# Two GNN layers on one core: rows from one scratch, and the adjacency over three DMA queues

## What is computed

```python
h = relu(layernorm(x))
mask = (adj > 0); deg = sum(mask, axis=1)
agg = mask @ h / max(deg, 1)
x = x + relu(concat([h @ W_self + b_self, agg @ W_nb + b_nb]) @ W_comb + b_comb)
h = relu(layernorm(x))
Wh = h @ W                      # 4 heads of 64
e = leaky_relu(sl[:, :, None] + sr.T[None], 0.2)    # sl, sr: Wh times a_l, a_r
alpha = softmax(where(mask | identity, e, -inf))
x = x + elu(alpha @ Wh)
```

## Time and profile before

| | us |
|---|---|
| median of 3 runs | 872.04 |
| lowest and highest | 863.84, 874.17 |
| profiled execution | 872.05 |
| its span, first to last instruction | 870.5 |
| PE, DVE, ACT, POOL busy | 799.2, 697.1, 564.1, 138.1 |

### The profile page before, as it was taken

One profiled execution on the slowest core, in us unless ns is written; L12 is line 12 of the kernel. 1 busy time (PEld: TensorE's weight loads), 2 busy tenths in 40 slices (PEclk: granted clock), 3 DMA queues, 4 the chain that ended last, 5 costly groups with the idle time before them and its releaser, 6 DMA issues.

```text
span 870.5 us, 26604 instructions
## 1 busy us (share of the span) xinstructions
PE 799.2 (92%) x10789; PEld 726.9 (84%) x10789; DVE 697.1 (80%) x1339; ACT 564.1 (65%) x839; POOL 138.1 (16%) x253
## 2 busy tenths in 40 slices
PE   5896898999999989969999999999999999999995
PEld 4342687778887878759999999999999999999995
DVE  3896766677776676587897999888999889998884
ACT  3574022222222222388999998999989999999991
POOL 0113234444444444400000000000000000000000
PEclk9999799999999999969999999999999999999998
DMA  8645999999999999440041012221101410112001
GB/s 212 181 145 142 281 277 289 285 307 318 316 304 296 300 298 295 101 107 26 1 96 48 2 47 49 49 49 47 48 6 43 96 48 8 41 49 48 9 16 37
DMA packets 91107, 115.68 MB, mean 133 GB/s; under 512 B 62608, under 2 KB 64464, under 8 KB 91056
## 3 DMA queue, kind: packets, MB, share of 16 engines
q1 hardware_dynamic: 70336, 61.57, 26.9%
q10 hardware_dynamic: 10784, 32.65, 13.5%
q0 software_dynamic: 9936, 20.86, 8.4%
HBM read 98.17 MB, written 16.85 MB: 132 GB/s over the span
## 4 chain that ended last, share of the span: by engine, by line
PE 39%; DVE 20%; DMA 17%; ACT 12%; issue 9%; POOL 1%; POOLq 0%; DVEq 0%; ACTq 0%
DMA rows<-own_scratch 14%; ACT stage L752 8%; PE ps_x L623 8%; PE ps_t L623 7%; PE ps_a L623 7%; PE ps_w L623 4%; PE ps_h L623 4%; DVE stage L1046 4%; DVE bits L940 2%; DMA stage<-in_adj 2%; DVE stage L1036 2%; PE ps_a L540 2%; DVE stage L1056 2%; PE ps_t L571 2%; PE ps_t L573 2%
## 5 line engine op out<-in xcount | busy, mean ns | idle before, releaser
L571 PE MATMUL ps_t<-g,mask 128*128 128x257 f16 x1024 | 230.3, 275 | 9.9 <-DVE mask L947 9.9
L573 PE MATMUL ps_t<-g,mask 128*128 128x256 f16 x1024 | 230.2, 273 | 0.0
L752 ACT ACTIVATE stage<-rows,sr 128x1024 int8<-128x1024 f32 x192 | 204.3, 1171 | 5.7 <-PE ps_w L623 5.7
L752 ACT ACTIVATE stage<-bits,sr 128x1024 int8<-128x1024 f32 x192 | 204.3, 1170 | 2.4 <-PE ps_w L623 2.4
L1046 DVE SCALAR_TENSOR_TENSOR stage<-stage,mask 128x1024 int32<-128x1024 int32 x128 | 156.9, 1225 | 22.1 <-ACT stage L752 21.4
L623 PE MATMUL ps_x<-g,stage 128*128 128x130 f16 x2048 | 158.7, 219 | 10.0 <-DVE stage L1056 4.8
L623 PE MATMUL ps_t<-g,stage 128*128 128x130 f16 x2048 | 158.4, 219 | 0.0
L623 PE MATMUL ps_a<-g,stage 128*128 128x130 f16 x2048 | 158.4, 219 | 0.0
L623 PEld LDWEIGHTS ps_x<-g,stage 128*128 128x128 fp8e4 x2048 | 127.4, 97 | 12.1 <-issue 12.0
L623 PEld LDWEIGHTS ps_a<-g,stage 128*128 128x128 fp8e4 x2048 | 127.3, 97 | 0.3
L623 PEld LDWEIGHTS ps_t<-g,stage 128*128 128x128 fp8e4 x2048 | 127.3, 97 | 0.2
(11 more groups left out here) (130 smaller groups left out, 838.9 us busy)
## 6 DMA issues: line engine op xcount, KB each, us to landing
stage<-in_adj SPq DMA_DIRECT2D x134, 256.0 KB, 7.4
stage<-in_adj ACTq DMA_DIRECT2D x122, 256.0 KB, 9.1
own_scratch<-mask POOLq DMA_DIRECT2D x16, 256.0 KB, 2.6
rows<-in_x POOLq DMA_DIRECT2D x128, 32.0 KB, 7.3
rows<-own_scratch POOLq DMA_DIRECT2D x32, 128.0 KB, 9.3
x_scratch<-late POOLq DMA_DIRECT2D x32, 128.0 KB, 7.3
bits<-s_scratch SPq DMA_DIRECT2D x8, 512.0 KB, 4.2
rows<-s_scratch SPq DMA_DIRECT2D x8, 512.0 KB, 4.7
```

The costliest lines, as they stand in the source:

```text
L571: nc.tensor.matmul(ps_t32[e][:, 0:D + 1], at, g[:, 2 * kk + b, D:2 * D + 1], start=kk + b == 0, stop=kk == NK - 1 and b == 1, skip_group_c ...
L573: last = nc.tensor.matmul(ps_t32[e][:, 0:D], at, g[:, 2 * kk + b, 0:D], start=False, stop=kk == NK - 1 and b == 1, skip_group_check=True)
L752: nc.scalar.activation(sign_bytes(sgn, k, b), srow[gr % 2], ACT.Sign, bias=sr[:, 2 * k + b, H + gr // NS:H + gr // NS + 1]).then_inc(act_s ...
```

## The change

- The own rows and x now lie in one scratch tensor `rows_d`, 2 KB for each partition and tile. POOL stores x into it in the first stage, a block at a time, from the buffers of x, beside own; SP refills a buffer of x only after that store.
- The row of a tile is one transfer of 256 KB in place of five.
- POOL's loop is written out; in each tile it stores wh of tile t-1, then x1 of tile t, then fetches the row of t+2.
- The adjacency: SP loads steps 3, 4 and 5 whole; from step 6 on SP loads parts 0 and 1, ACT part 2, and POOL part 3, at the end of its turn for the tile. Parts of steps 6 to 8 POOL issues ahead of its loop, after the last own stores have landed.
- `to_bits` waits for POOL's part on a semaphore of its own.

```diff
-    own_d = nc.dram_tensor("own_scratch", (NK, P, 2 * D), F32, kind="Internal").ap()
+    rows_d = nc.dram_tensor("rows_scratch", (NK, P, 2, 2 * D), F32, kind="Internal").ap()
...
-        rows = sb("rows", [P, 4, D], F32)
-        own = rows[:, 0:2, :]
-        xt = rows[:, 2:4, :]
+        rows = sb("rows", [P, 2, 2 * D], F32)
+        own = rows[:, :, 0:D]
+        xt = rows[:, :, D:2 * D]
...
                 sp.wait_ge(h_ready, k - XR + 1)
+                sp.wait_ge(x_out[k % XR], k // XR * 16)
                 x_rows(sp, k)
...
             for n in range(3, 2 * NT):
-                adj_rows(sp, n, range(UN // 2))
+                adj_rows(sp, n, range(UN if n < 6 else UN // 2))
...
+            def store_own(k):
                 pool.wait_ge(own_ready, k * 2 + 2)
+                pool.dma_start(rows_d[k, :, :, 0:D], ownA[:, k % 2, :].rearrange("p (e d) -> p e d", e=2)
+                               ).then_inc(own_out[k % 2], 16)
+
+            def store_x(k):
+                pool.wait_ge(x_in[k % XR], (k // XR + 1) * 16 * UN)
+                pool.dma_start(rows_d[k, :, :, D:2 * D], xin[k % XR].rearrange("p (e d) -> p e d", e=2)
+                               ).then_inc(x_out[k % XR], 16)
+
+            def row(t):
+
+                pool.dma_start(rows[:, t % 2, :], rows_d[t // 2, :, t % 2, :]).then_inc(row_in[t % 2], 16)
...
+            store_x(0)
+            store_x(1)
+            for k in range(NK - 2):
+                store_x(k + 2)
+                store_own(k)
             for b in range(2):
                 pool.wait_ge(own_out[b], 16 * (NP2 - 1))
+            for i in range(XR):
+                pool.wait_ge(x_out[i], 16 * NK // XR)
+            row(0)
+            row(1)
+            store_own(NK - 2)
+            store_own(NK - 1)
             for b in range(2):
                 pool.wait_ge(own_out[b], 16 * NP2)
+            def adj_part(n):
+
+                pool.wait_ge(bits_ready, n - 2)
+                pool.dma_start(halves[n % 3][(UN - 1) * UP:, :].rearrange("p (e c) -> p e c", e=2),
+                               adj_v[n // UN, n % UN, UN - 1]).then_inc(stage_in_pool[n % 3], 16)
+
+            for n in range(6, 9):
+                adj_part(n)
+            for t in range(NT):
+                if t:
+                    store_wh(t - 1)
+                store_x1(t)
+                if t + 2 < NT:
+                    row(t + 2)
+                for n in (2 * t + 9, 2 * t + 10):
+                    if n < 2 * NT:
+                        adj_part(n)
...
-            for n in range(3, 9):
-                adj_rows(act, n, range(UN // 2, UN))
+            for n in range(6, 9):
+                adj_rows(act, n, (2,))
...
                 if 2 * t + 9 < 2 * NT:
-                    adj_rows(act, 2 * t + 9, range(UN // 2, UN))
+                    adj_rows(act, 2 * t + 9, (2,))
                 high_h1T(t, t % 2)
                 if 2 * t + 10 < 2 * NT:
-                    adj_rows(act, 2 * t + 10, range(UN // 2, UN))
+                    adj_rows(act, 2 * t + 10, (2,))
...
-                dve.wait_ge(row_in[e], (k + 1) * 16 * (UN + 1))
+                dve.wait_ge(row_in[e], (k + 1) * 16)
```

More of the change, by code:

```diff
@@ L221, in build @@
         own_out = [sem(f"own_out{i}") for i in range(2)]
+        x_out = [sem(f"x_out{i}") for i in range(XR)]
         stage_in = [sem(f"stage_in{i}") for i in range(3)]
+        stage_in_pool = [sem(f"stage_in_pool{i}") for i in range(3)]
         row_in = [sem(f"row_in{i}") for i in range(2)]
@@ L436, in _ @@
             nc.gpsimd.tensor_copy(diag[:, :].rearrange("p (n e) -> p e n", e=2), diagf).then_inc(consts, 1)
-            def store_own(k, b):
+            def store_own(k):
                 pool.wait_ge(own_ready, k * 2 + 2)
[L441 to L461, removed]
-                pool.wait_ge(wh_ready, t + 1)
-                pool.dma_start(wh_d[bass.ds(t, 1)].rearrange("o p d -> p (o d)"), wh[:, e, :]
-                               ).then_inc(wh_out[e], 16)
+                pool.dma_start(rows_d[k, :, :, 0:D], ownA[:, k % 2, :].rearrange("p (e d) -> p e d", e=2)
+                               ).then_inc(own_out[k % 2], 16)
@@ new lines, in store_x, with store_x1 @@
+            def store_x(k):
[4 more added lines that the diff above has]
+                pool.dma_start(rows[:, t % 2, :], rows_d[t // 2, :, t % 2, :]).then_inc(row_in[t % 2], 16)
+            def store_x1(t):
+                pool.wait_ge(x1m_ready, t + 1)
+                pool.dma_start(x1_d[t], x1[:, t % 2, :]).then_inc(x1_out[t % 2], 16)
@@ L466, in _, with store_wh @@
+            def store_wh(t):
+                pool.wait_ge(wh_ready, t + 1)
+                pool.dma_start(wh_d[t], wh[:, t % 2, :]).then_inc(wh_out[t % 2], 16)
+            store_x(0)
[3 more added lines that the diff above has]
+                store_own(k)
             for b in range(2):
                 pool.wait_ge(own_out[b], 16 * (NP2 - 1))
[L468 to L471, removed]
+            for i in range(XR):
+                pool.wait_ge(x_out[i], 16 * NK // XR)
@@ L935, in to_bits @@
             def to_bits(n):
-                dve.wait_ge(stage_in[n % 3], (n // 3 + 1) * 16 * UN)
+                whole = min(n // 3 + 1, 2)
+                dve.wait_ge(stage_in[n % 3], whole * 16 * UN + (n // 3 + 1 - whole) * 16 * (UN - 1))
+                if n >= 6:
+                    dve.wait_ge(stage_in_pool[n % 3], (n // 3 - 1) * 16)
                 if n >= 2:
```

## The result

| | before | after |
|---|---|---|
| median, us | 869.77 (4 runs) | 898.56 (4 runs) |
| profiled span, us | 870.5 | 898.7 |

The ratio is 1.0337, 95% interval 1.0266 to 1.0407. The prediction was 860, with a range up to 880: wrong, and on the other side of no change.

What follows compares the result with a forecast made beforehand. The prediction took a two-tile loop through the row's transfer to bound the aggregation. It summed -8 us for POOL's adjacency loop and -4 at the aggregation's start to -12 on 872.05: 860 us, range 844 to 880.

Steps and rivals of the forecast that it cites:

- the row loop: Aggregation: x1 store, row transfers and landing, spanning two tiles, were claimed to explain the pace of 8.73 us a tile.
- the full DMA engines: Aggregation: the DMA engines, not the loop, set the pace, so only 3 us are gained, 869 us; chance 0.28.
- (a): Row fetch in the aggregation: one transfer for five lands at T + 13.2 to 15.2, so the row wait goes.
- (b): POOL's adjacency part behind the row: landing in 7.7 us, loop 16.8 us, 8.4 a tile, gaining 8 us.
- T + 6.5: POOL's issue of its part of step 2t+9, 6.5 us after L969 of tile t starts at T.
- Rival 3: POOL's longer queue in the aggregation becomes the late one: 881 us, 896 at a landing of 10.4; chance 0.14.
- (c): Store of wh ahead of x1 in the aggregation: ACT's 105.4 us wait goes, worth nought.
- (d): Start of the aggregation: SP loads step 3 whole earlier; tile 2 was put 4 us earlier, at 115.
- (e): Store of x in the first stage: cost bounded by 0 to 3 us, taken as 0.

Runs made afterwards that it cites:

- e1: The changed kernel with the adjacency back on two queues (SP parts 0 and 1, ACT 2 and 3, from step 3), none on POOL: 876.8 us, ratio 1.008.
- e10: e1 with the row fetched in five transfers again, own and four parts of x, all from the scratch: 867.9 us, ratio 0.997.
- e2: The kernel before with the three-queue adjacency and the change's wh order; row in five transfers, no store of x: 914.8 us, ratio 1.052.
- e4: The changed kernel with POOL's adjacency part of step 2t+9 issued ahead of the store of x1 and the row: 881.1 us, ratio 1.014.
- e7: e1 with ACT's part 3 moved to SP, so SP loads parts 0, 1 and 3, ACT only 2: 894.6 us, ratio 1.031.
- e8: The kernel before with wh stored ahead of x1 and POOL's loop written out; row in five transfers, x from the input: 867.8 us, ratio 0.998.
- e17: e1 with the row in four transfers of 32 partitions each, 2 KB pieces: 865.7 us, ratio 0.996.
- e5: e1 with destinations exchanged, SP loading parts 0 and 2, ACT 1 and 3: 893.9 us, ratio 1.033.
- e6: e5 with ACT's two parts in the other order, part 3 first, then part 1: 895.0 us, ratio 1.032.

## Why the prediction was wrong

- *What bounds the kernel.* Wrong. I read the row loop as the bound because its length fitted the pace, and the full DMA engines only as a rival (0.28). e1 and e10 decide: in e1 the row wait of 42.8 us goes, 47.8 of adjacency wait comes, the rate stays and the time does not fall; in e10 the two waits sum to 56.9 us against 55.8, at the same time. A chain whose links are DMA landings has the length that the engines' load gives it, so it fits whatever the bound is.
- *(a) The row wait goes.* Right (L978 has none), but it was worth nothing, and the single transfer costs 9 us with two queues (e1 against e10), which no part of the sum had.
- *(b) POOL's part.* This is the step that failed. "The landing, again bounded by 7.3 and 9.3 ... I take 7.7, nearer to the lower end, because ACT's queue loses half of its transfers": it was 10.4, outside the bounds. They came from POOL's queue with 640 KB a tile and could not hold for one with 1,024. (The gain of 8 us is also rounded down: 0.33 x 27 is 8.9.) The issue at T + 6.5 was right (203.22 against 196.97, T + 6.25). With 10.4, 6.25 + 10.4 + 2.6 is 19.25 for two tiles, 9.6 each; measured 9.84. Instead of 16.8 us the loop took over 19, and DVE waited 58.0 us at the bits. The landing is no constant of the queue: 9.4 in e2, 10.4 after, 11.8 in e4, which is the fastest of the three.
- *Rival 3* was the one that came, mechanism and place: decision from 8.6 on, 896 at 10.4, measured 898.6. It had 0.14, and its price in the range (881) was taken from the landing of 9.3, though its own argument said that the queue would be longer. Its account is only part of the cause: e4, which mends the place, is still 4 us behind e1 and 11 behind before, and e7 loses 18 us against e1 without POOL.
- *The assumption that the rate is given.* No term of the sum had a rate that falls with the spread over the queues, while the rows showed 237, 297 and 320 GB/s at one share of 1.03. I used that difference to argue that more could be moved; it also said that less could.
- *(c)* Nothing gained or lost by the wh order: right, by e8 (0.998, interval 0.994 to 1.001).
- *(d)* 4 us at the start: tile 0 came 3.4 earlier (97.43 against 100.85), but tile 2 only 1.1. Step 3 was there in time, as forecast. Steps 4 and 5 through SP alone were late by 1.79 and 5.71 us, and POOL's first part was issued at 95.58, as worked out (near 97):

```profile
87.48 1.23 DVE L949 TENSOR_SCALAR bits<-stage 128x2048 uint8<-128x2048 int32 x1 [1.79 <-DMA stage<-in_adj]
95.17 1.23 DVE L949 TENSOR_SCALAR bits<-stage 128x2048 uint8<-128x2048 int32 x1 [5.71 <-DMA stage<-in_adj]
...
95.58 1.98 POOL L482 DMA_DIRECT2D stage<-in_adj  x3 [9.23 <-issue]
```

- *(e)* The store of x is hidden: right (e10 against e8, 867.9 and 867.8).
- *The rule of the Trainium skill* ("DMA: Bandwidth & Descriptors", section "Issuing engines are not separate DMA queues"), that all issuing engines share the same DMA engines and several of them save only issue time, gave the right warning against a gain, but not the loss: the spread over the queues is not neutral here, 298 to 259 GB/s.

## What to carry to other kernels

Where the DMA engines are full, taking a DMA wait away moves it; first ask whether the bytes or the rate change. Treat the rate as something the schedule makes: of the six spreads over two queues or one tried here, equal shares, each queue kept to its own half of the partitions, gave the most, and the others lost 5 to 13% of the rate at an unchanged share. A transfer that another engine waits for belongs early in its queue's program (17 us by e4), and a landing time read off a queue is no bound for that queue with 60% more bytes.

## What was not expected of the hardware

- The DMA share is 1.02 or 1.03 in every run while the rate goes from 254 (e2) to 311 GB/s (e17): the share says that the engines are occupied, not what they achieve.
- One transfer of 256 KB over 128 partitions lost 9 us against five, and 11 against four of 32 partitions, to the same buffer from the same scratch (e1, e10, e17). The cause is open.
- Which quarter of the partitions a queue writes was worth 17 us (e5, e6 against e1), with the same number, size and order of transfers.
